# Attention of a four-stage kernel: scores as three fp32r products over head pairs, keys masked on GpSimd, keys projected before queries, VectorE's output block behind two maxima

## What is computed

```python
pairs = [(0, 0), (1, 0), (1, 1)]          # (branch, offset); SEG = 128
for br, off in pairs:
    xs = x[:, off::DIL[br], :].reshape(b_, -1, 128, 256)
    qkv = xs @ Wqkv[br].T + bqkv[br]       # 16 heads of 16
    scores = einsum('...qhd,...khd->...hqk', q, k) * 0.25
    o = einsum('...hqk,...khd->...qhd', softmax(scores), v)
    outs.append(o @ Wout[br].T + bout[br])
x = x + sum(outs) / 3                      # x came in through a layer norm
```

## Time and profile before

| | |
|---|---|
| Median of 3 runs | 4033.05 us (4030.51 to 4034.83) |
| Profiled execution, its own time | 4029.58 us |
| Its span in the trace | 4027.7 us |
| Busy: PE, DVE, ACT, POOL | 3816.6, 3206.9, 3074.0, 2282.1 us |
| Attention's 128 units, from the first scores | 1138.9 to 2200 us |
| PE, DVE, ACT, POOL busy in that stretch | 1039.84, 840.50, 917.06, 130.81 us |

### The profile page before, as it was taken

One profiled execution on the slowest core, in us unless ns is written; L12 is line 12 of the kernel. 1 busy time (PEld: TensorE's weight loads), 2 busy tenths in 40 slices (PEclk: granted clock), 3 DMA queues, 4 the chain that ended last, 5 costly groups with the idle time before them and its releaser, 6 DMA issues. The chain is left out here.

```text
span 4027.7 us, 82430 instructions
## 1 busy us (share of the span) xinstructions
PE 3816.6 (95%) x29464; PEld 3337.1 (83%) x29464; DVE 3206.9 (80%) x7740; ACT 3074.0 (76%) x7818; POOL 2282.1 (57%) x1818
## 2 busy tenths in 40 slices
PE   7999999999979999999998699999999997999999
PEld 6888888888768888888887588888888886898878
DVE  7888888888768787878776788888888876756677
ACT  6888888888778888888887688888888876633166
POOL 7888888888611111111100688888888875512266
PEclk8999999999989999999999899999999998999999
DMA  2000000000010000000000200000000002331342
GB/s 65 17 17 17 17 17 17 17 17 17 11 47 13 18 18 22 14 23 13 23 7 12 70 17 17 17 17 17 17 17 17 17 9 90 118 110 56 124 158 89
DMA packets 135063, 141.97 MB, mean 35 GB/s; under 512 B 8672, under 2 KB 131968, under 8 KB 134656
## 3 DMA queue, kind: packets, MB, share of 16 engines
q1 hardware_dynamic: 134656, 136.71, 10.6%
HBM read 80.06 MB, written 56.62 MB: 34 GB/s over the span
## 5 line engine op out<-in xcount | busy, mean ns | idle before, releaser
L300 POOL TENSOR_TENSOR f_grid<-f_sim 128x1024 f32<-128x1024 f32 x512 | 969.4, 1910 | 0.0
L1485 ACT ACTIVATE a_ex<-a_p_s,a_mneg 128x128 f32<-128x128 f32 x2048 | 728.3, 410 | 144.0 <-DVE a_mneg L1539 144.0
L686 DVE SCALAR_TENSOR_TENSOR f_p_u<-f_grid,f_te,f_p_dot 128x1024 f32<-128x1024 f32 x512 | 654.0, 1277 | 111.5 <-PE f_p_dot L106 65.1
L308 POOL TENSOR_TENSOR f_q<-f_q 128x1024 f32<-128x1024 f32 x256 | 607.9, 2386 | 123.7 <-ACT f_q L558 121.3
L695 DVE SCALAR_TENSOR_TENSOR f_q<-f_p_u,f_rz,f_grid 128x1024 f32<-128x1024 f32 x512 | 651.9, 1273 | 0.4
L539 ACT ACTIVATE f_grid<-f_grid,f_negm 128x1024 f32<-128x1024 f32 x512 | 559.7, 1144 | 0.0
L1485 ACT ACTIVATION_READ_ACCUMULATOR a_ex<-a_p_s,a_mneg 128x1 f32 x2048 | 510.0, 249 | 0.0
L443 PE MATMUL f_p_y<-f_eup,f_wT 128*128 128x256 f32 x2048 | 472.8, 379 | 0.0
L438 PE MATMUL f_p_y<-f_wdn,f_hs 128*128 128x256 f32 x2048 | 468.4, 382 | 0.0
L443 PEld LDWEIGHTS f_p_y<-f_eup,f_wT 128*128 128x128 f32 x2048 | 388.5, 190 | 57.7
L438 PEld LDWEIGHTS f_p_y<-f_wdn,f_hs 128*128 128x128 f32 x2048 | 378.8, 190 | 49.7
(11 more groups left out here) (623 smaller groups left out, 10456.7 us busy)
## 6 DMA issues: line engine op xcount, KB each, us to landing
x_f<-f_yt SPq DMA_DIRECT2D x64, 256.0 KB, 2.2
f_xt<-x SPq DMA_DIRECT2D x32, 256.0 KB, 2.9
a_xt<-x_f SPq DMA_DIRECT2D x16, 512.0 KB, 3.8
x_a<-a_yt SPq DMA_DIRECT2D x16, 512.0 KB, 2.9
f_xt<-x_a SPq DMA_DIRECT2D x32, 256.0 KB, 2.9
c_xt<-x_f SPq DMA_DIRECT2D x16, 512.0 KB, 4.7
x_c<-c_yt SPq DMA_DIRECT2D x16, 512.0 KB, 3.2
b1p_xt<-x_c SPq DMA_DIRECT2D x16, 512.0 KB, 3.9
```

What stands on the lines that cost most here:

```text
L300: g_grid.mark(pool.tensor_tensor(grid[v][:, hd, :].rearrange("p (i j) -> p i j", i=XROWS), sx[:, hd, :].unsqueeze(2).to_broadcast([P, XROW ...
L308: g_pair.mark(pool.tensor_tensor(q[v][:, 2 * k, :], q[v][:, 2 * k, :], q[v][:, 2 * k + 1, :], ALU.add), f"{v}{k}")
L686: d_mask.mark(dve.scalar_tensor_tensor(out=p_u[:], in0=grid[v][:, hd, :], scalar=te[:, v, hd, TOP - 1:TOP], in1=p_dot[:], op0=ALU.is_ge, o ...
L1485: last = act.activation(ex[t.step % 2][:, i, n, :], p_s[i][:, n, :], ACT.Exp, bias=mneg[:, i, n:n + 1], accum_out=z[t.step % 2][:, i, n:n ...
```

## The change

Queries are stored once, as a high and a low fp32r part (`qT`), keys masked to each parity, high and low (`kz`). A score is three fp32r products, low times high twice and high times high, added up in PSUM, each against 256 columns (both parities of a key half). ScalarE now writes each projection twice, in full (`full`) and as its high part; GpSimd subtracts for the low part and multiplies key parts with the parity column. Keys are j = 0, 1 and queries j = 2, 3. VectorE's `put_out` and `inverse` go behind the first two maxima, and TensorE's `turn_rz` behind the transposes of quad 0.

```diff
-        qz = [m.sbuf(f"qz{br}", DC, 2, S) for br in range(BR)]
-        kT = [m.sbuf(f"kT{br}", DC, S) for br in range(BR)]
+        qT = [[m.sbuf(f"qT{br}{k}", DC, S, dt=F32R) for k in "hl"] for br in range(BR)]
+        kz = [[m.sbuf(f"kz{br}{k}", DC, 2, S, dt=F32R) for k in "hl"] for br in range(BR)]
+        full = [m.sbuf(f"full{k}", S) for k in range(2)]
+        k_hi, k_lo = [m.sbuf(f"k{k}h", S, dt=F32R) for k in range(2)], m.sbuf("kl", S, dt=F32R)
...
+                def split_qk(t):
+                    br, j = ur_of(t) // SEGS, t.step % SEGS
+                    c, x = j % DC, full[t.step % 2]
+                    a_qk.wait(pool, t)
+                    if j >= DC:
+                        hi, lo = (a[:, c, :] for a in qT[br])
+                        g_qk.mark(pool.tensor_tensor(lo, x[:], hi.bitcast(F32), ALU.subtract))
+                        return
+                    hi = k_hi[t.step % 2]
+                    k_mark = Turn(t.group, t.step // SEGS * DC + j, ROWS * UR // 2)
+                    if (t - 1).exists():
+                        g_qk.wait(pool, t - 1)
+                    g_kl.mark(pool.tensor_tensor(k_lo[:], x[:], hi[:].bitcast(F32), ALU.subtract))
+                    for n, part in enumerate((hi, k_lo)):
+                        if n:
+                            g_kl.wait(pool, k_mark)
+                        for e in range(2):
+                            last = pool.tensor_tensor(kz[br][n][:, c, e, :], part[:].bitcast(F32),
+                                                      par[:, e:e + 1].to_broadcast([P, S]), ALU.mult)
+                    g_qk.mark(last)
...
                 scale(first_row + 1)
+                pool.wait_ge(s_p, 16 * 4)
+                for j in range(AHEAD):
+                    split_qk(first_unit + j)
                 pool.wait_ge(s_b, 4)
                 biased(first_row)
...
+                    if (t + AHEAD).exists(last=units):
+                        split_qk(t + AHEAD)
                     if u == 7 and (r + 1).exists(last=rows):
                         biased(r + 1)
...
                     if j == 0:
-                        a_qk.wait(pe, t + (SEGS - 1))
+                        g_qk.wait(pe, t + (SEGS - 1))
...
                     for c in range(DC):
-                        for e in range(2):
+                        for n, (q, k) in enumerate(((0, 1), (1, 0), (0, 0))):
                             for i in range(QUAD):
                                 lanes = slice(i * SLOT, (i + 1) * SLOT)
-                                mm = pe.matmul(p_s[i][:, 2 * c + e, :], qz[br][lanes, c, e, j * P:(j + 1) * P],
-                                               kT[br][lanes, c, j * P:(j + 1) * P], start=True, stop=True)
-                                if (c, e) == (DC - 1, 1):
+                                mm = pe.matmul(p_s[i][:, 2 * c:2 * c + 2, :], qT[br][q][lanes, c, j * P:(j + 1) * P],
+                                               kz[br][k][lanes, c, :, j * P:(j + 1) * P], start=n == 0, stop=n == 2)
+                                if (c, n) == (DC - 1, 2):
                                     t_s.mark(mm, str(i))
...
                     c = j % DC
+                    if (t - 2).exists():
+                        g_qk.wait(act, t - 2)
...
+                    for out in (full[t.step % 2][:], hi):
+                        last = act.activation(placed(out, br), natural(p_pr[:], br), ACT.Identity, bias=bias, scale=scale)
                     a_qk.mark(last)
```

More of the change, by code:

```diff
@@ L1173, in dilated_attention @@
         s_hi, s_lo, s_p = m.sem("s_hi"), m.sem("s_lo"), m.sem("s_p")
-        SETUP = 4
+        SETUP = 3
         quads = [str(b) for b in range(QUAD)]
@@ L1433, in step @@
                         value(t + SEGS)
+                    turn_ex(t, 0)
                     if before:
                         turn_rz(t - 1)
-                    turn_ex(t, 0)
-                    if before:
                         attend(t - 1)
@@ L1464, in project @@
                     c = j % DC
[L1465 to L1468, removed]
-                    else:
-                        last = act.activation(placed(kT[br][:, c, :], br), natural(p_pr[:], br), ACT.Identity,
-                                              bias=bk[:, br, c:c + 1])
+                    if (t - 2).exists():
+                        g_qk.wait(act, t - 2)
+                    if j >= DC:
+                        hi, bias, scale = qT[br][0][:, c, :], bqs[:, br, c:c + 1], HD ** -0.5
+                    else:
+                        hi, bias, scale = k_hi[t.step % 2][:], bk[:, br, c:c + 1], 1.0
+                    for out in (full[t.step % 2][:], hi):
+                        last = act.activation(placed(out, br), natural(p_pr[:], br), ACT.Identity, bias=bias, scale=scale)
                     a_qk.mark(last)
@@ L1590, in evict, with evict_rest @@
                         turn_h(next_row, part)
+                def evict_rest(t):
+                    u, r = ur_of(t), row_of(t)
                     if (r - 1).exists():
@@ L1624, in _ @@
                 dve.wait_ge(s_p, 16 * 4)
-                dve.tensor_scalar(qs[:], par[:], HD ** -0.5, None, ALU.mult).then_inc(s_c, 1)
                 dve.tensor_copy(bvr[:], bv[:].unsqueeze(3).to_broadcast([P, BR, DC, P]))
-                dve.wait_ge(s_c, SETUP - 1)
-                for e in range(2):
-                    last = dve.tensor_scalar(bqs[:, e], bq[:], qs[:, e:e + 1], None, ALU.mult)
-                last.then_inc(s_c, 1)
+                dve.tensor_scalar(bqs[:], bq[:], HD ** -0.5, None, ALU.mult).then_inc(s_c, 1)
                 lower(1)
@@ L1662, in step @@
                         evict(t - 1)
+                    maximum(t, 0)
+                    maximum(t, 1)
+                    if before:
+                        evict_rest(t - 1)
                         inverse(t - 1)
-                    maximum(t, 0)
-                    if before:
                         turned(t - 1, 3)
-                    maximum(t, 1)
                     if u == 1 and (r + 2).exists(last=rows):
@@ L1671, in step @@
                         means(r + 2)
+                    maximum(t, 2)
                     if before:
                         turned_rz(t - 1)
-                    maximum(t, 2)
                     maximum(t, 3)
@@ L1682, in _ @@
                 evict(last_unit)
+                evict_rest(last_unit)
                 inverse(last_unit)
```

7 lines of the change are left out of this document (3 added, 4 removed).

## The result

The changed kernel took 4044.68 us, the median of 9 runs (4039.20 to 4050.11); the kernel before took 4034.83 (4027.77 to 4037.00) beside it, also in 9. The ratio is 1.0027, with a 95% interval of 1.0016 to 1.0037: slower by 6 to 15 us, where a small gain of 6 had been predicted. The profiled execution took 4039.20 us, the quickest of the nine, with a span of 4037.1.

What follows compares the result with a forecast made beforehand. The prediction took the attention unit's loop as the bound, with ScalarE's exponentials waiting for VectorE's maximum. Its terms, -44 + 31 + 7 = -6 us, gave 4023.6 us profiled and 4027 us as a median, range 4003 to 4050.

Steps and rivals of the forecast that it cites:

- -44: Attention units: the first maximum starts earlier, 40 us over 112 steady units and 4 us over 16 of rows 0 and 15.
- +31: Rows 1 to 13: GpSimd's key half delays `biased` and its load; VectorE's statistics wait, 2.4 us a row.
- +7: Opening: first scores wait for GpSimd's key halves through ScalarE's copies, at 1146.0 against 1138.91; bounds 6 and 9 us.
- A steady unit gains 0.36: VectorE: first maximum starts at 1705.02 in place of 1705.38, with block and reciprocal behind two maxima and shorter scores permitting it.
- ScalarE's copies and the turned sums, 0: Steady unit: doubled key copies and turning the sums behind quad 0 cost 0, at worst 0.1 us per unit.
- (a): Rival: the load is not late, so only gain and opening stand, 3996 us; chance 0.12.
- (b): Rival: fp32r row tiles overlap less, so scores are longer; 4048 us, or 4270 if tiles take turns; chance 0.13.
- (c): Rival: GpSimd slower than its rows, key half 6.35 us plus slower landing, making the load later; 4046 us; chance 0.22.
- the four cases: The three rivals and the prediction's own reckoning, net small, 4010 to 4040 us, chance 0.50; 0.03 left for something unseen.

Runs made afterwards that it cites:

- b2: Kernel before the change, unchanged, profiled a second time: 4029.98 us; second feed-forward to the end 1806.8 us, against 1802.8 in its first trace.
- e1: Kernel before the change with only the new order on VectorE and TensorE, float32 scores kept: 4021.13 us against 4030.86, 0.9976.
- e2: Changed kernel with the old order on VectorE and TensorE, split fp32r scores kept: 4063.54 us, 1.0078 of the kernel before.
- e3: Changed kernel with `biased` moved ahead of the key half in GpSimd's step u = 7: 4011.19 us, 0.9950 of the kernel before.
- e7: Changed kernel, load still late, both halves of VectorE's statistics moved behind the fourth maximum and `turned(t, 0)`: 4016.78 us, 0.9956 of the kernel before.
- e6: Changed kernel with three more unused 128x256 GpSimd products between the key half and `biased`: 4080.11 us, 1.0116 of the kernel before.
- e8: Changed kernel with 11 filler products on TensorE during its stall behind the late load: 4035.42 us against 4031.24 for the kernel before, 1.0014.
- e9: Changed kernel with `biased` ahead of the key half and the opening's two key halves on VectorE, masks using a column: 4005.06 us, 0.9937 of the kernel before.

## Why the prediction was wrong

The ledger of the profiled execution, from the stage's start to the last unit, against the -44, +31 and +7 of the prediction: gains -34, first units +33, opening +7, and +1.7 between the first scores and the first reciprocal, which adds up to some 8 (the two traces say 7.7) where -6 was expected. Of the 1.7, 1.2 are only the place from which units are counted: the reciprocal stands at S + 2.42 now, behind two maxima, and at S + 1.23 before. The last interval, with no maxima behind it, gives that back within the 34. The whole execution is 9.6 slower; the rest lies in the spread that b2 shows. Two things turn the sign of the sum: 10 us of gain that did not come, and 9 us of half clock behind the late load, a term that stood at nothing. With only one of them the sum would be -1 or -2.

**The gain, -44: the step that failed.** "A steady unit gains 0.36: 112 of them 40 us". It gained 0.30: 104 units of rows 1 to 13 at 0.305 are 31.7 us (reckoned: 37), rows 14 and 15 gave 2.2 and row 0 0.35 (reckoned for these 24 units: 7), in all 34. Of the 10 us that are missing, 5.7 are 0.05 us a unit and 4.3 are rows 0, 14 and 15, 1.4 of them the clock of the last interval. The places in the unit were read rightly (maximum at S + 1.03, scores hidden), and the 0.36 is what the maximum's start moved by. What was assumed is that the exponential follows it at the same distance. It follows at 0.77 instead of 0.72. The maximum itself is longer when it stands behind the low part: 0.68 us against the 0.63 that it took behind the reciprocal. The medians over each trace are 0.681 behind the low part in the changed kernel and 0.692 in e1, and 0.628 and 0.629 behind the reciprocal in the kernel before and in e2. e1 and e2 differ from their base in the order and show that the length goes with it. Why isn't shown: that the low part reads PSUM is not enough, since the maximum behind the statistics, which read SBUF, took 0.67 too.

**The late load, +31: a second step that failed, inside a right amount.** The mechanism is shown from both sides: without the late load (e3) the loss is gone, without the urgent work behind it (e7) nearly gone, with a later load (e6) larger. But the amount came out right because two errors met. The wait is 2.0 us long, and the six undisturbed first units are 9.90 us, 1.87 above 8.03: 24.3 us for thirteen, not 31.2. The key half took 5.25 us and not 5.55 (1.25 and 4 x 1.00), which is most of the difference. In its place came 8.9 us that the prediction did not have: seven first units with the lower clock, 11.18 on average against 9.90. That the stall brings it is shown by e8, e3 and e7. The Trainium skill, TensorE: Matmul & The Clock Gate, "HAM oscillation — how this bites in real kernels", tells of a wait for a DMA that lets TensorE's clock fall so that the work behind it starts slow. The waits of its example last 3 to 5 us. Here the clock fell in seven and eight of thirteen rows with stalls of 1.4 to 1.8 us, and 0.2 to 2.2 us after TensorE had begun again.

**The opening, +7: right by two parts that cancel.** The first scores came at 39.6 us behind the stage's start against 32.4, 7.2 later. GpSimd's second key half ended 33.4 us behind the start and not 34.7, and the scores followed it by 6.2 us and not 4.8. In between TensorE's granted clock was the lower one, where the kernel before had the full one:

```profile
1132.70:1143.00 10.30, 7.54 (x20) 6.00 (x21) 0.00 (x0) 3.42 (x7) 7.91 (x8) 0.50 0.00 1
```

```profile
1133.50:1138.91 5.41, 5.33 (x27) 4.16 (x25) 0.00 (x0) 2.66 (x5) 0.00 (x0) 1.00 0.00 0
```

With the key halves off GpSimd (e9, which has `biased` moved too) 5.1 of the 7.2 are gone. What the other 2.1 are was not taken apart.

**ScalarE's copies and the turned sums, 0.** No engine waits for GpSimd in the table of waits from 1160 to 2150 us, and the 0.31 us that the first exponential comes nearer to the scores' start (1.80 against 2.11) is the whole gain of the unit.

**The rivals.** (a), the load not late: no, but e3 is what it would have been, 0.9950 where it gave 0.991. Of the difference of some 16 us, 10 are the smaller gain of the unit; the others, at the stage's two ends, were not taken apart. (b), fp32r tiles that overlap less: refuted. Behind the first round of 0.22 us, four products of 256 columns fit in each 0.12 us. The 24 products, 2.9 us one by one, take 0.81, which is 3.6 times, and 4 behind the first round. The 3.07 times that the Trainium skill, TensorE: Matmul & The Clock Gate, "Measured speedup vs the span model", gives for four row tiles would have made it an estimated 0.94; the trace doesn't bear that out. But the scores end 0.06 us later than reckoned and so are hidden with nothing to spare. (c), GpSimd slower than its rows: refuted, it was quicker. The slow side was reached by another way, the clock. (The chances of the four cases add up to 0.38, 0.33 and 0.26; the 0.03 for something unseen all went to "slower" and was not shared.)

**What is left open.** The median lies 9.85 us above that of before, and the two traces of the changed kernel have the stage 7.7 and 15 us longer; the last row's clock makes the difference between them. Why it falls in more units of some executions than of others isn't shown, nor how many of the nine runs it slowed; what picks the rows that lose the clock behind the stall isn't either.

## What to carry to other kernels

When work is added to an engine that is mostly idle, look at what stands behind it in that engine's queue: `biased` released a load, and 5.25 us ahead of it cost what the rest of the change gained, while the same work put behind it (e3) kept the whole gain of the units. Add the clock to the price of a new stall on the busiest engine: a wait of 2 us cost 1.9 in six rows and 3.1 in seven. Look at the granted clock in every stretch of the changed kernel, not only at the place of the stall: the last row lost it in every trace with both edits. A step that gains only together with another should be costed as a pair, and the distance between two instructions read again for the instruction that will then stand ahead.

## What was not expected of the hardware

- TensorE's granted clock fell to 0.50 for 3.4 us, 0.2 to 2.2 us behind the end of a stall of 1.4 to 1.8 us, in 7 and 8 of 13 rows; with the stall filled, in 1 of 13; with stalls of 3.1 to 5.1 us, in 13 of 13.
- In the last row, without such a stall, it fell in one to four units in each of the nine traces with both edits, and in none of the four others.
- GpSimd's four scaled pieces of 128x256 took 4.86 to 4.89 us alone, 7.89 beside VectorE's operations on two SBUF tensors, and 6.57 where the masks, four of each five of those operations, took one tensor and a column. The Trainium skill, GPSIMD Engine Reference, tells in its table of specifications that GpSimd shares its SBUF interfaces with VectorE and contends with two-input instructions there; the traces agree and add the price.
- A GpSimd product of a 128x512 tensor with a broadcast column takes 1.00 us when the next follows directly (2.04 for two), a difference of two full tensors 1.25.
- VectorE's maximum of 128x512 from PSUM took 0.63 us behind the reciprocal, 0.68 or 0.69 behind the low part, which reads PSUM, and 0.67 behind the statistics, which read SBUF.
